# Graph network and attention on one core: the last state is turned by DMA, the s2 row comes through memory, and every engine gets a side table of its own

## The reference, cut to what matters

```python
h = maximum(layernorm(x), 0)
for i in range(3):                                  # layer 0
    m = einsum('bnd,de->bne', h, weight[i])
    aggr = einsum('bst,bsd->btd', A, m)
    h = gru_cell(aggr, h, w_ih, w_hh, b_ih, b_hh)   # r, z, n = two sigmoids and a tanh
x = x + h                                           # the residual
h = maximum(layernorm(x), 0)                        # layer 1
Wh = einsum('bnf,of->bno', h, W)
s1, s2 = Wh @ a1, Wh @ a2
e = leaky_relu(s1[:, :, None] + s2[:, None, :], 0.2)
att = masked_softmax(e, adj)
x = x + einsum('bij,bjo->bio', att, Wh)
```

## Time and profile before

| what | value |
|---|---|
| median of 3 runs | 1812.73 us (1812.6 to 1813.08) |
| the profiled execution's own time | 1811.33 us |
| its span, first to last instruction | 1809.5 us |
| PE busy | 1778.9 us |
| DVE busy | 1420.0 us |
| ACT busy | 1021.6 us |
| POOL busy | 350.2 us |
| mean granted clock of PE | 0.994 of full speed |

### The profile page before, as it was taken

One profiled execution on the slowest core, in us unless ns is written; L12 is line 12 of the kernel. 1 busy time (PEld: TensorE's weight loads), 2 busy tenths in 40 slices (PEclk: granted clock), 3 DMA queues, 4 the chain that ended last, 5 costly groups with the idle time before them and its releaser, 6 DMA issues.

```text
span 1809.5 us, 32208 instructions
## 1 busy us (share of the span) xinstructions
PE 1778.9 (98%) x10500; PEld 944.1 (52%) x10500; DVE 1420.0 (78%) x2827; ACT 1021.6 (56%) x1824; POOL 350.2 (19%) x758
## 2 busy tenths in 40 slices
PE   7999999999999999999999999999999999999995
PEld 5444555545555454555545555454554545555453
DVE  7668788787887877878787887878878777887877
ACT  5556555655555555555555556556556565556553
POOL 2022130311303122130311303113031221303100
PEclk9999999999999999999999999999999999999997
DMA  4223332423323223332332314223232332323121
GB/s 124 61 61 71 65 79 55 99 60 67 91 39 101 58 59 92 70 75 57 84 73 60 94 38 110 52 64 93 59 86 52 84 72 64 75 58 93 31 58 53
DMA packets 323712, 128.38 MB, mean 71 GB/s; under 512 B 239200, under 2 KB 323680, under 8 KB 323680
## 3 DMA queue, kind: packets, MB, share of 16 engines
q1 hardware_dynamic: 323680, 127.97, 30.0%
HBM read 52.96 MB, written 16.78 MB: 39 GB/s over the span
## 4 chain that ended last, share of the span: by engine, by line
PE 96%; DVE 1%; issue 1%; POOLq 0%; POOL 0%; ACT 0%; DVEq 0%
PE r_bank L332 28%; PE z_bank L332 27%; PE hn_bank L332 14%; PE in_bank L332 14%; PE s_bank L332 3%; PE w_bank L332 3%; PE nb_bank L346 2%; PE nb_bank L347 2%; PE t_bank L813 1%; PE t_bank L824 1%; DVE u_lo L1215 0%; DVE dot_terms L1169 0%; DVE x_out L1125 0%; DVE tail_max L1200 0%; DVE vt_lo L1114 0%
## 5 line engine op out<-in xcount | busy, mean ns | idle before, releaser
L917 ACT ACTIVATE n_out<-n_pre,bih 128x512 f32<-128x512 f32 x192 | 138.0, 719 | 239.9 <-DVE n_pre L1022 239.6
L926 ACT ACTIVATE ht_s<-ht 128x512 f16<-128x512 f32 x128 | 80.6, 630 | 265.1 <-DVE ht L1038 265.1
L332 PE MATMUL hn_bank<-ht_s,wh_hi 128*128 128x512 f16 x768 | 228.4, 379 | 1.7 <-PEq L447 1.7
L332 PE MATMUL r_bank<-ht_s,wh_hi 128*128 128x512 f16 x768 | 228.6, 379 | 0.0
L332 PE MATMUL z_bank<-ht_s,wh_hi 128*128 128x512 f16 x768 | 228.4, 379 | 0.0
L365 DVE TENSOR_TENSOR nb_lo<-nb_bank,nb_hi 128x512 f16<-128x512 f32 x192 | 131.2, 683 | 84.4 <-ACT nb_hi L361 84.3
L1017 DVE SCALAR_TENSOR_TENSOR n_pre<-tanh_r,hn_b 128x512 f32<-128x512 f32 x192 | 146.8, 764 | 61.8 <-ACT tanh_r L912 56.9
L309 POOL TENSOR_TENSOR ln_gnn<-stats_gnn 128x4 f32<-128x4 f32 x32 | 18.6, 580 | 887.8 <-DVE stats_gnn L260 887.8
L912 ACT ACTIVATE tanh_r<-r_bank,b_rz,down 128x512 f32<-128x512 f32 x192 | 147.0, 766 | 65.8 <-PE r_bank L332 65.8
L907 ACT ACTIVATE hn_b<-hn_bank,b_hn,down 128x512 f32<-128x512 f32 x192 | 147.7, 769 | 56.8 <-PE hn_bank L332 56.8
L1031 DVE SCALAR_TENSOR_TENSOR diff<-ht,n_out 128x512 f32<-128x512 f32 x192 | 132.0, 687 | 38.0 <-ACT n_out L917 37.7
(11 more groups left out here) (248 smaller groups left out, 3936.1 us busy)
## 6 DMA issues: line engine op xcount, KB each, us to landing
x_in<-in_x_dram SPq DMA_DIRECT2D x32, 512.0 KB, 4.0
x_res<-in_x_dram SPq DMA_DIRECT2D x32, 512.0 KB, 4.3
out_dram<-x_out SPq DMA_DIRECT2D x30, 512.0 KB, 5.3
adj_in<-in_adj_dram SPq DMA_DIRECT2D x32, 256.0 KB, 4.1
adj_att<-in_adj_dram SPq DMA_DIRECT2D x32, 256.0 KB, 4.5
h_s<-ht_s SPq DMA_TRANSPOSE x128, 3.0
ht_s<-h_s SPq DMA_TRANSPOSE x64, 3.2
out_dram<-x_out SPq DMA_DIRECT2D x4, 256.0 KB, 2.2
```

The costliest lines, as they stand in the source:

```text
L332: last = nc.tensor.matmul(bank_ap, w, d, start=start and i == 0, stop=stop and i == len(todo) - 1)
L917: nc.scalar.activation(n_out[c][:], n_pre[c][:], ACT.Tanh, bias=bih[:, 4 + c:5 + c]).then_inc(n_ready, 1)
L926: nc.scalar.activation(ht_s[layer % 2][a][:, c, 0, :], ht[a][:, c, :], ACT.Copy, scale=HSCALE).then_inc(ht_hi_ready, 1)
```

## The change

1. `residual` leaves PE for all pairs but the last. A new stage `split_last` makes f16 parts of the last state (ACT and DVE, as `split_state` does), `turn_last` (SP) turns them by DMA into `h_last`, `add_last` (POOL, 128x512) adds the two parts to `h_node`, and DVE adds `h_node` to `x_res` with one `scalar_tensor_tensor`. Its second input was in PSUM and is now in SBUF.
2. The s2 row leaves PE. `store_s2` writes s2 (128x4) to memory and `load_s2` reads it back into `s2_row`, broadcast over all partitions, both from SP's queue. ACT makes the sum s1 + s2 with four operations of 128x128; DVE's addition goes.
3. `SIDE` becomes one table per engine. DVE's `dots` has a new wait for `relu_att`.

The last slot of the last pair and the tail are as before.

```diff
+    "act": {
+        (0, 2): [("split_last", 1, 1, -1), ("apply_att", 0, -1), ("neighbours", 1, 0, 0, 0)],
...
+        (1, 5): [("neighbours", 0, 1, 1, 0), ("apply_att", 1, -1)],
...
+    "dve": {
+        (0, 0): [("update", 1, 2, 1, -1), ("dots", 0, 0, -1)],
+        (0, 1): [("dots", 0, 1, -1)],
+        (0, 2): [("split_last", 1, 1, -1)],
+        (0, 3): [("neighbours", 1, 0, 0, 0), ("update", 0, 0, 0, 0)],
...
+        (1, 3): [("update", 1, 0, 0, 0), ("dots", 1, 0, -1), ("split_state", 1, 1, 0, 0)],
+        (1, 4): [("neighbours", 0, 1, 1, 0)],
...
                 def turn_last(p, a, c):
+                    if not after_gates(p):
+                        sp.wait_ge(last_lo_ready, per_chunk(p, a, c))
+                        sp.sem_inc(sp_step, 1)
+                        wait_reached(sp, h_node_ready, per_chunk(p, a, c) - 2)
+                        sp.sem_inc(sp_step, 1)
+                        sp.dma_start_transpose(h_last[:, c].rearrange("p s b t -> p (s b) t"),
+                                               ht_s[LAYERS % 2][a][:, c].rearrange("p s t -> p (s t)")).then_inc(
+                                                   h_last_landed[a][c], 16)
+                def store_s2(p, a):
+                    sp.wait_ge(dots_ready, per_group(p, a))
+                    sp.dma_start(s2_dram[a], s2[a][:]).then_inc(s2_stored[a], 16)
+                def load_s2(p, a):
+                    sp.wait_ge(s2_stored[a], per_load(p))
+                    wait_reached(sp, sum_ready, per_group(p, a) - 1)
+                    sp.dma_start(s2_row[:].rearrange("q t b -> q (t b)"),
+                                 s2_dram[a].rearrange("t b -> (t b)").unsqueeze(0).broadcast_to(
+                                     [P, T])).then_inc(s2_landed[a], 16)
...
                 def residual(p, a, c):
+                    if not after_gates(p):
+                        return
...
-                def scores(p, a):
-                    pe.wait_ge(dots_ready, per_group(p, a))
...
-                    for b in range(GROUP):
-                        last = nc.tensor.transpose(t_bank[:, b * P:(b + 1) * P],
-                                                   s12[a][:, b, 1:2].broadcast_to([P, P]), ident[:])
...
+                def split_last(p, a, c):
+                    if not after_gates(p):
+                        act.wait_ge(h_ready, per_gate(p, a, LAYERS - 1, c))
+                        nc.scalar.activation(ht_s[LAYERS % 2][a][:, c, 0, :], ht[a][:, c, :],
+                                             ACT.Copy, scale=HSCALE).then_inc(last_hi_ready, 1)
...
+                def scores(p, a):
+                    act.wait_ge(s2_landed[a], per_load(p))
+                    wait_reached(act, minus_max_ready, per_group(p, a) - 1)
+                    for b in range(GROUP):
+                        last = nc.scalar.activation(score[:, b, :], s2_row[:, :, b], ACT.Identity,
+                                                    bias=s1[a][:, b:b + 1])
+                    last.then_inc(sum_ready, 1)
...
+                    if not after_gates(p):
+                        dve.wait_ge(h_node_ready, per_chunk(p, a, c))
+                        nc.vector.scalar_tensor_tensor(part, h_node[c][:], 1.0 / HSCALE, part, ALU.mult,
+                                                       ALU.add).then_inc(x1_ready, 1)
+                        return
...
                 def dots(p, a, half):
+                    dve.wait_ge(relu_att_ready, per_group(p, a))
...
                 def whole_state(p, a, c):
                     pool.wait_ge(first_ht_landed[a][c], per_load(p))
-                    wait_reached(pool, res_t_done, per_chunk(p - 1, a, c))
+                    wait_reached(pool, last_lo_ready, per_chunk(p - 1, a, c))
...
+                def add_last(p, a, c):
+                    if not after_gates(p):
+                        pool.wait_ge(h_last_landed[a][c], per_load(p))
+                        wait_reached(pool, x1_ready, per_chunk(p, a, c) - 2)
+                        nc.gpsimd.tensor_tensor(h_node[c][:], h_last[:, c, 0], h_last[:, c, 1],
+                                                ALU.add).then_inc(h_node_ready, 1)
```

More of the change, by code:

```diff
@@ L59 @@
 SIDE = {
[L60 to L101, removed]
@@ L102 @@
[L102 to L104 removed]
+    "pe": {
+        (0, 4): [("neighbours", 1, 0, 0, 0)],
+        (0, 5): [("residual", 1, 0, -1), ("neighbours", 1, 0, 1, 0)],
+        (1, 2): [("scores", 0, -1)],
+        (1, 3): [("neighbours", 0, 1, 0, 0)],
+        (1, 6): [("neighbours", 0, 1, 1, 0)],
+        (2, 0): [("residual", 1, 1, -1)],
+        (2, 1): [("neighbours", 1, 1, 0, 0)],
+        (2, 7): [("neighbours", 1, 1, 1, 0)],
+        (3, 0): [("gather", 0, 0, -1)],
+        (3, 2): [("neighbours", 0, 2, 0, 0)],
+        (3, 4): [("gather", 0, 1, -1)],
+        (3, 5): [("neighbours", 0, 2, 1, 0), ("attend", 0, 0, -1)],
+        (3, 7): [("scores", 1, -1)],
+        (4, 1): [("attend", 0, 1, -1), ("neighbours", 1, 2, 0, 0)],
+        (4, 5): [("neighbours", 1, 2, 1, 0)],
+        (4, 7): [("gather", 1, 0, -1)],
+        (5, 1): [("gather", 1, 1, -1), ("neighbours", 0, 0, 0, 1), ("residual", 0, 0, 0)],
+        (5, 2): [("residual", 0, 1, 0)],
+        (5, 5): [("neighbours", 0, 0, 1, 1), ("attend", 1, 0, -1)],
+        (5, 6): [("attend", 1, 1, -1)],
+    },
@@ L622, in graph_blocks @@
         u_lo = both("u_lo", [P, GROUP, D], F16)
-        s12 = both("s12", [P, GROUP, 2], F32)
+        s1 = both("s1", [P, GROUP], F32)
+        s2 = both("s2", [P, GROUP], F32)
+        s2_row = sb("s2_row", [P, P, GROUP], F32)
+        s2_dram = [nc.dram_tensor(f"s2_dram{a}", [P, GROUP], F32, kind="Internal").ap() for a in range(2)]
         row_scale = both("row_scale", [P, GROUP], F32)
@@ L634, in graph_blocks @@
         diff = [sb(f"diff{c}", [P, T], F32) for c in range(2)]
+        h_last = sb("h_last", [P, KC, 2, GROUP, P], F16)
+        h_node = [sb(f"h_node{c}", [P, GROUP, P], F32) for c in range(KC)]
         score = sb("score", [P, GROUP, P], F32)
@@ L701, in graph_blocks, with slots @@
         inv_ready, row_scale_ready, out_ready = sem("inv_ready"), sem("row_scale_ready"), sem("out_ready")
-        def slots(p, gate, side):
+        def slots(p, gate, side, table):
             for slot in range(2 * LAYERS):
@@ L708, in slots, with all_pairs @@
                     last_slot = slot == 2 * LAYERS - 1 and not exists(p + 1)
-                    for stage, *which, offset in (LAST_SLOT_SIDE if last_slot else SIDE).get((slot, step), ()):
+                    for stage, *which, offset in (LAST_SLOT_SIDE if last_slot else table).get((slot, step), ()):
                         if stage in side and exists(p + offset):
                             side[stage](p + offset, *which)
-        def all_pairs(engine, gate, side):
+        def all_pairs(engine, gate, side, table):
             for stage, *which in HEAD:
@@ L716, in all_pairs @@
                     side[stage](0, *which)
-            slots(0, gate, side)
+            slots(0, gate, side, table)
             with engine.Fori(1, pairs - 1) as p:
-                slots(p, gate, side)
-            slots(pairs - 1, gate, side)
+                slots(p, gate, side, table)
+            slots(pairs - 1, gate, side, table)
             for stage, *which in TAIL:
```

159 lines of the change are left out of this document (129 added, 30 removed).

## The result

The changed kernel takes **1831.76 us** (median of 5 runs, 1830.19 to 1832.16), the kernel before 1812.62 us on the same chip (1811.67 to 1813.08). The ratio is 1.0104 (95% interval 1.009 to 1.0119): slower by 19.1 us, where the prediction has 8.4. The time lies in the range and in the case that I forecast, but the forecast took less than half of the movement.

The account below looks back on a forecast made before the run. PE's queue was taken to bound the pairs. Stalls of 3.4 us against 2.85 us won gave +0.55 us a pair, times 15 = +8 us, so 1821 us; the range that leaves out 2 in 10 was 1787 to 1834.

Parts of the forecast that it names:

- the case that I forecast: Slower, 1816 to 1833 us, by DVE's wait for relu_att before dots plus POOL's additions; 42 in 100.
- What bounds the kernel, and what leaves PE: PE's queue bounds the pairs, 109.37 us each; removed transposes and a 0.24 us wait give 2.85 us a pair.
- ACT, DVE, POOL and SP as load: Added work per pair, ACT at most 6.7 us, DVE +1.4 us, costed at nothing because PE's 106 us hide it.
- Place A: Slot 0, neighbours of chunk 1: PE 0.45 us late, 1.4 taken with a meeting of POOL and DVE.
- Place C: Slot 2, neighbours of group 1, chunk 0: the turn by DMA lands 1.35 us late for PE.
- Place B: Slot 1, r gate, nb_lo of chunk 1: late through two meetings of POOL and DVE, bounds 0 and 1.15, 0.6 taken.
- Place D: Slot 2's r gate of chunk 0, a place that the prediction doesn't have.
- the list of stalls in the sum: Three late places for PE, 3.4 us a pair against 2.85 us won: +0.55 us, times 15 = +8 us.
- With all: Upper value with every meeting of POOL and DVE: stalls of 3.95 us a pair, +16.5 us, 1829 us.
- The rule on the meetings: DVE instructions with two SBUF inputs and GpSimd instructions reading SBUF exclude each other; residual exposed too, 1829 us.
- The stalls are there, the meetings are not: Rival: POOL's additions fall on DVE operations that read a bank; 1797 us, 1788 to 1809; 25 in 100.
- All is hidden: Rival: turns and relu_att come sooner than added up; 1770 us, up to 1788 with small stalls; 13 in 100.

Follow-up runs that it names:

- the version with all moves and the fill: Changed kernel with both dots and u_lo later on DVE, add_last filling zeros except in 16 columns: 1770.5 us, ratio 0.9759.
- the best version: Changed kernel with both groups' dots and u_lo of group 0 later on DVE, same instructions: 1774.86 us, ratio 0.9788.
- both fills: Changed kernel with POOL's add_last and whole_state filling zeros instead of adding, except in 16 columns: 1805.23 us, ratio 0.9951.

## Why the prediction was right or wrong

**What bounds the kernel, and what leaves PE: right.** A pair without stalls is 106.52 us by the prediction, and the version with all moves and the fill has just that; the one with the transposes put back has 108.28, four groups of 0.44 more. The gain of 2.85 us a pair is real.

**ACT, DVE, POOL and SP as load: right at nothing.** ACT's busy time grew by 91.5 us, DVE's by 85.6 and POOL's by 63.7 against the earlier trace rows, and the best version carries all of it under PE. DVE's growth is mostly not the new work, which the prediction put at 1.4 us a pair, but the meetings: with both fills it is busy for 1411.9 us, less than before. The two DMAs of the s2 row delay nothing in these traces.

**Place A: right, a little low.** Forecast 1.4 with the meeting, 0.45 without; measured 1.61, and 0.67 without (both additions fill). The meeting itself was 0.97 us against the 0.95 of the earlier trace rows. Moving the dots takes A away. No run parts the wait in front of these dots from their own 2.8 us. +0.2 us.

**Place C: right.** Forecast 1.35 (1.4 in the sum), measured 1.25, and the turn landed 3.07 us after its issue, as before. The cause is mostly the wait in front of dots, which the run with an earlier relu_att shows. But "the chain's start is PE itself" is half of it. PE's last product of these neighbours ends at 1052.99 in the pair above, and ACT's tanh_r, the end of a run that holds the new sums, lets nb_hi start at 1053.03: two ways of equal length meet there, and where ACT's became the longer one (u_lo alone moved), D grew to 0.97.

**Place B: right in mechanism, too small.** "Bounds 0 and 1.15; I take 0.6, between them, since the landing can slip past n_pre." It did not slip: the two additions followed each other on split_state and on n_pre, and the wait stands in 14 of the 15 pairs, all but pair 1. Measured 0.75. Both u_lo in front and the meeting of add_last are needed for it: either one taken away removes B. +0.15 us.

**Place D: not in the sum.** After place C, I stopped at the DMA. The same late DVE has nb_lo of chunk 1 behind split_state (1057.61 in the pair above), and slot 2's r gate needs it before the neighbours need the turn. 0.34 us, of the same cause: it went both where these dots were moved and where their wait was shortened.

**The step that failed is the list of stalls in the sum.** The walk found "three places" and added "1.4 + 0.6 + 1.4 = 3.4 us against 2.85 us won": it is four places, 1.61 + 0.75 + 0.34 + 1.25 = 3.95. The largest missing term is place D, 0.34 us that the prediction put at nothing; A was 0.21 and B 0.15 too small, C 0.15 too large. The mechanism was right. But the balance of a pair, 0.55, is a small difference of two large terms, so 0.6 us missed in it doubles it: +1.15 us a pair measured, 15 x 0.6 = 9 us. The prediction's upper value, "With all: 1.4 + 1.15 + 1.4 = 3.95", gives 1829 and was nearly right by luck: it has B too large by 0.4 and no D.

**Pair 1 and the clock.** The profiled spans differ by 19.8 us, 2.5 more than 15 x 1.15. Pair 1 holds 2.2 of them: it grew by 3.4 us (109.17 to 112.54) and not by 1.15. The rest of the kernel, from the last slot on, takes the same 51.4 us in both. In pair 1 PE waits longer at A, and its next products are slow:

```profile
148.78 0.23 PE L429 MATMUL nb_bank<-adj_s,h_s 128*128 128x128 f16 x1 [2.54 <-DVE nb_lo L448]
...
150.01 0.63 PE L415 MATMUL in_bank<-nb_hi,wi_lo 128*128 128x512 f16 x1
150.44 0.63 PE L415 MATMUL in_bank<-nb_hi,wi_hi 128*128 128x512 f16 x1
```

From one product to the next are 0.43 us instead of 0.22: the granted clock of PE is 0.50 from 149.3 to 152.6, the lower of its two levels (1.2 GHz), where the kernel before has 1.00. The in and z gates take 5.57 us instead of 3.88, so this one stall cost its length and 1.7 us more. The 1.46 us at A in the pair shown further up left the clock at 1.00. A wait of 2.54 us doesn't always do it: the run with relu_att earlier has one too, at 150.46, and stays at 1.00. What decides is open, and so is why A is longer in pair 1.

**The choice for place B.** I took the middle between bounds for B with nothing in the trace for the lower one: the landing had been worked out (16.3), and it lay in front of split_state.

**The rule on the meetings.** DVE and POOL take turns for whole instructions here: 1.64 against 0.69 us, in split_state, n_pre, `diff` and the products of dots alike, and none of split_state once POOL only fills. That is what the Trainium skill states (SBUF — State Buffer, section Who interferes with whom), also in the part that an instruction of GpSimd that only writes doesn't contend. By that rule the prediction gave 1829, and the trace agrees. Only its reason, the exposed residual, is not what happened: `x_res` took 0.68 to 0.69 us in all of its 60 times, so it met no addition.

**Rivals.** "The stalls are there, the meetings are not" (1797) is what the version with both fills is: 1804 by the ratio, 7 more, which are D and the 0.67 at A where 0.45 was forecast, less 0.1 at C. "All is hidden" (1770 to 1788) is what the change becomes with a few entries of its tables moved (1775).

## What to carry to other kernels

When work is moved off the bounding engine, count first which instruction now stands *waiting* at the head of an in-order queue, and what is behind it: here dots and its wait for relu_att alone, without a meeting, cost PE some 35 us (both fills, 1804, against the 1769 by the ratio of the version with no stall in its pairs), and moving a few entries behind what PE needs turned +1% into -2%. An operation with slack goes behind the ones with a due time, not to where its input is likely to be ready. And where the balance is a difference between a known gain and a sum of stalls, follow each late engine to every consumer before taking a middle value: a place taken off such a path alone, as u_lo was, gives nothing, since the delay appears at the next place.

## What the runs showed of the hardware that was not expected

- A meeting costs both sides. POOL's addition of 128x512 took 1.34, 1.60 and 1.63 us instead of 1.15 when DVE was in the middle of an instruction with two SBUF inputs, and two in a row on each side alternate without a gap.
- The short products of dots meet too: 0.42 us becomes 1.39, the largest factor of all, since the stop is about as long (0.97 us) as the 0.95 of an operation of 0.69.
- ACT's sums of 128x128 take 1.66 us of the chain for four, 0.42 each. The prediction had each between nothing and 0.58. In the best version they cost PE nothing, though they stand in ACT's run in front of relu_att.
- A stall of 2.54 us of PE in pair 1 was followed by 3.3 us at granted clock 0.50, and one just as long in another run was not.
